# A Mamba and mixture-of-experts block on one core: another order of engines and steps in the first stage

## The reference

```
m = mean(x);  v = var(x);  xn = (x - m) / sqrt(v + eps)
```

```
logits = tokens @ Wg;  gates = softmax(logits);  idx = argmax(gates)
locations = cumsum(one_hot(idx)) - 1        # place in the expert's list; kept if < 1024
out[t] = gate[t] * (relu(tokens[t] @ W1[e] + b1[e]) @ W2[e] + b2[e])   # for kept tokens
```

## Time and profile before

| | |
|---|---|
| median of 3 runs | 1117.55 us (1115.28 to 1118.39) |
| the profiled execution's own time | 1116.6 us |
| its span, first to last instruction | 1114.8 us |
| VectorE busy | 1009.5 us (91%) |
| TensorE busy | 973.8 us (87%) |
| GpSimd busy | 880.4 us (79%) |
| ScalarE busy | 756.5 us (68%) |
| granted TensorE clock, mean | 0.939 of full speed |
| first scan of the first unit starts | 77.12 us after the span's start |

### The profile page before, as it was taken

The page is one execution under the profiler, slowest core; times in us unless marked ns, Lnnn a source line. Parts: engine busy times, 40 slices in busy tenths (PEclk is TensorE's granted clock), DMA queues, the critical chain, the costliest instruction groups (busy, mean ns, idle before and its releaser), DMA issues.

```text
span 1114.8 us, 11984 instructions
## 1 busy us (share of the span) xinstructions
PE 973.8 (87%) x3529; PEld 446.0 (40%) x3529; DVE 1009.5 (91%) x1358; ACT 756.5 (68%) x1219; POOL 880.4 (79%) x774
## 2 busy tenths in 40 slices
PE   6676777999999998989999999999899999788785
PEld 3332232444444444434444443444344444334232
DVE  5458897999999999999999999999999999999995
ACT  5655445777777868877777878678777768576331
POOL 3527888888888889798988888889889898788753
PEclk9787968999999999999999999999999999898767
DMA  9365335442342254353325324335333232945500
GB/s 275 110 152 162 79 86 128 97 101 43 84 113 64 68 116 85 76 123 76 86 48 116 80 53 114 84 76 123 85 69 81 50 85 57 216 96 113 132 29 10
DMA packets 77452, 106.99 MB, mean 96 GB/s; under 512 B 8734, under 2 KB 46540, under 8 KB 77388
## 3 DMA queue, kind: packets, MB, share of 16 engines
q1 hardware_dynamic: 72944, 97.74, 39.6%
q0 software_dynamic: 4096, 8.46, 2.2%
q10 hardware_dynamic: 348, 0.03, 0.0%
HBM read 17.99 MB, written 21.10 MB: 35 GB/s over the span
## 4 chain that ended last, share of the span: by engine, by line
PE 34%; DVE 22%; ACT 16%; issue 15%; POOL 11%; DMA 0%; POOLq 0%; DVEq 0%; ACTq 0%
DVE u_sb L1005 9%; DVE s_sb L1048 8%; PE bank L1189 5%; PE bank L1226 5%; POOL s_sb L636 5%; PE bank L1154 4%; PE bank L1134 4%; PE bank L1241 4%; PE bank L1219 4%; POOL expert_in L643 4%; ACT bank L860 3%; PE bank L1186 3%; PE bank L1145 2%; ACT L719 2%; ACT L715 2%
## 5 line engine op out<-in xcount | busy, mean ns | idle before, releaser
L636 POOL TENSOR_TENSOR s_sb<-s_sb,c_of 128x512 f32<-128x512 f32 x480 | 614.5, 1289 | 127.9 <-DVE s_sb L1048 123.2
L1048 DVE TENSOR_TENSOR_SCAN s_sb<-bank,u_sb 128x512 f32<-128x512 f32 x512 | 619.9, 1211 | 15.1 <-ACT bank L860 14.9
L860 ACT ACTIVATE bank<-bank,a_neg 128x510 f32<-128x510 f32 x512 | 332.3, 664 | 213.4 <-PE bank L1226 211.7
L1005 DVE TENSOR_TENSOR u_sb<-bank,b_of 128x512 f32<-128x512 f32 x512 | 342.5, 669 | 25.8 <-PE bank L1219 25.3
L1219 PE MATMUL bank<-dsp,sel_d 128*128 128x512 f32 x512 | 329.8, 644 | 24.6 <-DVE u_sb L1005 18.7
L1226 PE MATMUL bank<-dsp,sel_d 128*128 128x512 f32 x512 | 230.1, 449 | 50.6 <-DVE s_sb L1048 47.0
L1219 PEld LDWEIGHTS bank<-dsp,sel_d 128*128 128x128 f32 x512 | 101.2, 198 | 204.0 <-DVE u_sb L1005 108.0
L1226 PEld LDWEIGHTS bank<-dsp,sel_d 128*128 128x128 f32 x512 | 101.3, 198 | 177.4 <-DVE s_sb L1048 132.4
L1241 PE MATMUL bank<-s_sb,con 128*32 128x512 f32 x1024 | 145.1, 640 | 24.6 <-POOL s_sb L636 21.8
L1134 PE MATMUL bank<-xnT,wx 128*128 128x512 f32 x256 | 133.7, 607 | 0.0
L643 POOL DMA_INDIRECT expert_in<-xn,put_at x64 | 65.3, 1021 | 38.9 <-DVE put_at L1034 21.1
(11 more groups left out here) (140 smaller groups left out, 1032.7 us busy)
## 6 DMA issues: line engine op xcount, KB each, us to landing
b_of<-bc SPq DMA_DIRECT2D x64, 256.0 KB, 5.5
c_of<-bc SPq DMA_DIRECT2D x64, 256.0 KB, 5.8
dsp<-hi SPq DMA_DIRECT2D x64, 256.0 KB
dsp<-dd SPq DMA_DIRECT2D x64, 256.0 KB
expert_in<-fill SPq DMA_DIRECT2D x16, 260.0 KB, 5.9
xn<-expert_in SPq DMA_DIRECT2D x8, 520.0 KB, 5.3
moe<-fill SPq DMA_DIRECT2D x8, 512.0 KB, 7.1
xn<-L_ffn_W SPq DMA_DIRECT2D x16, 256.0 KB, 5.0
```

The costliest lines, as they stand in the source:

```text
L636: pool.tensor_tensor(s_now, s_now, c_of[:, hf, hh, :], ALU.mult).then_inc(S["p_ready"], 1)
L860: act.activation(d, d, ACT.Exp, scale=a_neg[:, k:k + 1]).then_inc(S["decay_ready"], 1)
L1005: dve.tensor_tensor(u_sb[:, w % U_RING, :], du_ps[w % 2][:, :], b_of[:, hf, head_of(w), :], ALU.mult).then_inc(S["u_ready"], 1)
L1048: dve.tensor_tensor_scan(s_sb[:, w % S_RING, :], decay_of(w)[:, :], u_sb[:, w % U_RING, :], 0.0, ALU.mult, ALU.add).then_inc(S["scan_done" ...
```

## The change

In the layer norm, ScalarE takes the logarithm and exponential of group 1 ahead of the first SiLUs, and those of the other groups as early as their variances allow; it norms one chunk (11) instead of five. GpSimd norms chunks 1 to 10 and 12, VectorE chunks 0 and 13 to 15. The copies of chunks 6, 8, 10, 12 and 14 to `xnT` go to VectorE. TensorE transposes one or two chunks earlier than before, and `logits(q)` waits for each chunk's copy by itself. ScalarE's exponential of the routing stands behind the second half's SiLUs. TensorE makes the two routing products ahead of the second half's bc and v tiles, and its first spreads wait for `rt_pos` (the fifth signal of `route_dve`) in place of `routed`. VectorE forms the gates' sum and reciprocal behind the integer copy of the places.

```diff
+NORM_BY = ("dve",) + ("pool",) * 10 + ("act", "pool", "dve", "dve", "dve")
+XNT_BY_DVE = (6, 8, 10, 12, 14)
+FIRST_DX = 12
...
+        def normed(j):
+            name = NORM_BY[j]
+            return S["xn_" + name], sum(NORM_BY[i] == name for i in range(j + 1))
+        def taken(j):
+            if j in XNT_BY_DVE:
+                return S["xnT_dve"], XNT_BY_DVE.index(j) + 1
+            return S["xnT_act"], sum(i not in XNT_BY_DVE for i in range(j + 1))
...
-            for g in range(1, LN_GROUPS):
-                if g == LN_GROUPS - 1:
+            for j in range(1, CHUNKS):
+                if NORM_BY[j] != "pool":
+                    continue
+                pool.wait_ge(S["rstd_ready"], [a <= j * CT for a in LN_AT].count(True))
+                for i in range(j * CT, (j + 1) * CT):
+                    ins = norm(pool, i)
+                ins.then_inc(S["xn_pool"], 1)
+                if j == FIRST_DX:
                     scale_x(0, 0)
-                pool.wait_ge(S["rstd_ready"], g + 1)
...
+                    pool.wait_ge(S["dx_ready"], 1)
+                    zero_first()
...
             act.wait_ge(S["setup_act"], 5)
+            rsqrt(1)
             silus(0, 0)
-            rsqrt(1)
+            rsqrt(2)
...
             take_bc(0, 0)
-            norm_tiles(1)
             taps(1, 5)
+            rsqrt(3)
...
-            rsqrt(2)
             evac(wo.rearrange("p k m -> p (k m)"), y_ps[:, 2 * P:4 * P], 7)
             softplus_step(0, 0, 1)
-            norm_tiles(2)
             take_xnT(1)
+            rsqrt(4)
             softplus_step(0, 0, 2)
             take_xnT(2)
-            rsqrt(3)
             softplus_step(0, 0, 3)
             take_xnT(3)
-            norm_tiles(3)
+            rsqrt(5)
             take_xnT(4)
+            take_xnT(5)
+            copy_logits(0)
+            norm_tiles(11)
             take_delta(0, 0)
-            copy_logits(0)
-            rsqrt(4)
-            take_xnT(5)
-            take_xnT(6)
-            norm_tiles(4)
             take_xnT(7)
             copy_logits(1)
-            rsqrt(5)
-            take_xnT(8)
+            split_high(0, 0)
             take_xnT(9)
-            norm_tiles(5)
-            take_xnT(10)
-            split_high(0, 0)
             take_xnT(11)
             copy_logits(2)
-            for j in range(12, CHUNKS):
-                take_xnT(j)
+            take_xnT(13)
+            take_xnT(15)
             copy_logits(3)
+            silus(0, 1)
             act.wait_ge(S["lg_read"], CHUNKS // 4)
             act.activation(rt_b, rt_a, ACT.Exp).then_inc(S["route_act"], 1)
-            silus(0, 1)
...
+            def take_xnT(j):
+                dve.wait_ge(S["xnT_pe"], j + 1)
+                dve.tensor_copy(xnT[:, SEQS * j:SEQS * (j + 1), TAPS - 1:ROW],
+                                xnT_bank(j)[:, :].rearrange("p (s t) -> p s t", s=SEQS)).then_inc(S["xnT_dve"], 1)
...
-                if g == 5:
-                    take_logits(0)
             newton(LN_GROUPS - 1)
             dve.wait_ge(S["rstd_ready"], LN_GROUPS)
-            norm_tiles(CHUNKS - 1, 2)
-            for q in range(1, 4):
-                take_logits(q)
+            norm_tiles(13, 2)
+            norm_tiles(14, 3)
+            norm_tiles(15, 4)
+            take_xnT(6)
+            take_logits(0)
+            take_xnT(8)
+            take_xnT(10)
+            take_logits(1)
+            take_xnT(12)
+            take_xnT(14)
+            take_logits(2)
+            take_logits(3)
...
-            dve.wait_ge(S["route_act"], 1)
-            link(dve.tensor_reduce(r_sum, by_e(rt_b), AX, ALU.add))
-            link(dve.reciprocal(r_sum, r_sum))
...
-            link(dve.tensor_tensor(rt_pos, du_ps[0][:, :], rt_scan, ALU.add))
-            dve.wait_ge(S["route_dve"], 4)
+            dve.tensor_tensor(rt_pos, du_ps[0][:, :], rt_scan, ALU.add).then_inc(S["route_dve"], 1)
+            dve.wait_ge(S["route_dve"], 5)
...
-            link(dve.tensor_copy(r_place, r_code))
+            dve.tensor_copy(r_place, r_code)
+            dve.wait_ge(S["route_act"], 1)
+            link(dve.tensor_reduce(r_sum, by_e(rt_b), AX, ALU.add))
+            dve.reciprocal(r_sum, r_sum)
...
             transposes(4)
+            transposes(5)
             logits(0)
+            transposes(6)
             pe.wait_ge(S["sel_ready"], 1)
             first_tile("D", 0)
-            transposes(5)
-            transposes(6)
             by_token(0)
             transposes(7)
+            transposes(8)
             logits(1)
-            transposes(8)
...
             transposes(12)
+            transposes(13)
             by_token(2)
-            transposes(13)
             transposes(14)
             transposes(15)
             logits(3)
             by_token(3)
             first_tile("z", 1)
             first_tile("x", 1)
-            first_tile("bc", 1)
-            first_tile("v", 1)
-            pe.wait_ge(S["xnT_act"], CHUNKS)
             pe.wait_ge(S["route_dve"], 4)
             pe.matmul(du_ps[1][:, :], ones, rt_hot[:, :, 0:TILES], start=True, stop=True).then_inc(S["route_pe"], 1)
             pe.matmul(du_ps[0][:, :], tri, rt_hot[:, :, 1:TILES + 1], start=True, stop=True
                       ).then_inc(S["route_pe"], 1)
-            pe.wait_ge(S["routed"], 1)
+            first_tile("bc", 1)
+            first_tile("v", 1)
+            pe.wait_ge(S["route_dve"], 5)
             for w in range(AHEAD):
                 spread(0, w)
```

More of the change, by code:

```diff
@@ L230, in bass_mamba_moe @@
             "wt_ready a_by_d_ready sel_ready setup_pe setup_act fill_zeroed fill_ready ein_filled moe_filled "
-            "xn_dve xn_act xn_pool xnT_pe xnT_act logits_pe route_dve route_act route_pe routed "
+            "xn_dve xn_act xn_pool xnT_pe xnT_act xnT_dve logits_pe route_dve route_act route_pe routed "
             "l0_ready stats_done var_ready rstd_ready ln_act lt_pe lt_act lg_read "
@@ L583, in split_low @@
                 pool.tensor_tensor(lo, dd, hi.bitcast(F32), ALU.subtract).then_inc(S["lo_ready"], 1)
-            for g in range(1, LN_GROUPS):
-                if g == LN_GROUPS - 1:
-                    scale_x(0, 0)
-                pool.wait_ge(S["rstd_ready"], g + 1)
[L589 to L595, removed]
+            for j in range(1, CHUNKS):
[6 more added lines that the diff above has]
+                if j == FIRST_DX:
+                    scale_x(0, 0)
+                    pool.wait_ge(S["dx_ready"], 1)
+                    zero_first()
             split_low(0, 0)
@@ L695, in take_xnT, with norm_tiles @@
                                ACT.Copy).then_inc(S["xnT_act"], 1)
-            def norm_tiles(g):
-                act.wait_ge(S["rstd_ready"], g + 1)
-                for i in range(LN_AT[g], LN_AT[g] + CT):
+            def norm_tiles(j):
+                act.wait_ge(S["rstd_ready"], [a <= j * CT for a in LN_AT].count(True))
+                for i in range(j * CT, (j + 1) * CT):
                     ins = act.activation(xn[:, i, :], acc[:, i, :], ACT.Identity, bias=shift[:, i:i + 1],
@@ L1083, in transposes @@
             def transposes(j):
[L1084 to L1089, removed]
+                pe.wait_ge(*normed(j))
                 if j > 3:
-                    pe.wait_ge(S["xnT_act"], j - 2)
+                    pe.wait_ge(*taken(j - 3))
                 elif j > 0:
@@ L1104, in logits @@
                     pe.wait_ge(S["lt_act"], q)
-                pe.wait_ge(S["xnT_act"], 4 * (q + 1))
                 for k in range(4):
                     j = 4 * q + k
+                    pe.wait_ge(*taken(j))
                     mm = pe.matmul(lt_ps[32 * k:32 * (k + 1), :], wg_sb[:, :],
```

## The result

The changed kernel takes 1101.07 us (median of 4 runs, 1099.94 to 1102.15) against 1117.16 of the kernel before in the same comparison (4 runs): a ratio of 0.986, 95% interval 0.9848 to 0.9872, or 16 us. The forecast was 9 us, and 1104.5 to 1113 as the range. The direction was right, the size was not.

A forecast was written before the change was run, and what follows sets the result against it. First stage taken as a relay with no leading engine, then GpSimd's scatters. x tile 6.4 us earlier and tail 2.6 bring the first scan 8.9 us earlier: 1116.6 to 1107.7, with 0.95 for the median, rounded to 1108.5; range 1104.5 to 1113.

The forecast's parts named there:

- Logarithms, scales and norms: First stage's layer norm: group 1's scale at 17.0 us instead of 21.1, and no norm late for its transposes.
- The D tile, not the norms, is next: First half's D tile: the norms' early lead yields only 1.2 us, D ending at 39.1 against 40.3.
- Relay 15.6: From the D tile's end to the second half's z tile: 15.6 us, including 2.6 for a low clock.
- T to the first scan: 9.2: From the end of the second half's x tile (T) to the first scan: 9.2 us, 2.6 better than before.
- The first scan's lead passes through: Behind the first scan: the distance to the end stays 1037.7 us, so its 8.9 us lead shortens the whole.
- the high clock: Rival: no low clock stretch behind the D tile, gain 11.5 us, 1106 us; chance 0.11.
- The other three: Rivals: low clock for more of the relay, 1112, 0.13; GpSimd's norms slowed beside VectorE, 1117, 0.06; all low clock, 1122.5, 0.04.
- the slower one: Rival: TensorE at 1.2 GHz from the D tile to the v tile, first scan 4.8 us late, 1122.5; chance 0.04.
- about 85%: In the slower rival: share of the stretch at the low clock level from which the change costs time.

The follow-up runs named there:

- e3: Kernel before with four idle matmuls of 384 columns, two behind transposes(2) and two behind transposes(3): 1115.9 us, ratio 1.0001.
- e10: Changed kernel with the routing's exponential ahead of the second half's SiLUs and the gates' sum and reciprocal ahead of the scan of places again: 1102.8 us.
- e7: Changed kernel with ScalarE norming five chunks again (1, 4, 7, 10 and 13): 1105.3 us, ratio 0.9898 to the kernel before.
- e9: Changed kernel with logits(q) waiting for all four copies before its first product, as before: 1102.3 us, ratio 0.9884 to the kernel before.
- e1: Kernel before with only the end of the stage (the tail) changed: 1113.0 us, ratio 0.997.
- e2: Changed kernel with the end of the stage (the tail) put back as before: 1103.9 us, ratio 0.9883 to the kernel before.
- e5: Kernel before with 14 idle matmuls of 384 columns in TensorE's gaps: 1112.4 us, ratio 0.9966.
- e6: Kernel before with only the logarithms of groups 1 to 5 at the changed kernel's places: 1114.8 us, ratio 0.9987.
- e8: Changed kernel with all 16 copies on ScalarE: 1103.3 us, ratio 0.9876 to the kernel before.
- e12: Changed kernel with the exponential and gates' sum early again and three idle matmuls between the second and third spread: 1100.4 us, ratio 0.9856 to the kernel before.

## Why the prediction failed, step by step

- *Logarithms, scales and norms.* Right. Group 1's Newton step at 16.17 (forecast 16.1), GpSimd's 44 tiles from 17.14 on in 19.41 us (forecast 17.0 and 0.43 a tile). No norm was late.
- *"The D tile, not the norms, is next", ending at 39.1.* This step failed, and most. Its working took TensorE's prices from the rows of before, which were taken at 1.2 GHz, for a stretch that the changed kernel ran at 2.4 GHz. The forecast was 31.4 for the start of `logits(0)`, then 1.9, 1.0 for `transposes(6)` and 4.8 for the D tile. Measured: 30.48, then 1.9, 0.5 and 3.0, so 35.89. `logits(0)` starts 0.9 us sooner by the waits by chunk and takes no less, as it waits inside for its last copy. With the forecast's own start and the prices of full clock (1.0 from e3, 0.5, 3.0) the sum is 35.9: all of the 3.2 us is the clock. With the clock at 0.51 the same stream ended the D tile at 38.00 (e10), only 1.1 below the forecast, so 2.1 of the 3.2 us are the luck of this execution.
- *Relay 15.6.* The same step failed by 3.8 us here. It put 2.6 us for a low clock ("the new order feeds TensorE with shorter gaps, so I take 2.6"). That term measured nothing: in all profiles of the new order but e7's (0.97) the clock is 1.00 from 36 to 58 us, and the relay is 11.8 wherever norms, copies and waits are those of the change. The other 1.2 us: I summed the lengths of rows, and rows of pipelined matmuls overlap. Two transposed chunks took 1.04 us where I put 1.2, and a `by_token` that doesn't wait 0.44 and not 0.66. e9 gives 0.4 of it to the waits by chunk.
- *T to the first scan: 9.2.* Nearly right, 9.4; the tail 13.88 for 13.5. e1 and e2 show its 2.35 us by themselves. One reason in it was wrong: the exponential isn't on the path (e10).
- *The first scan's lead passes through.* Right: the rest is 1036.5 against 1037.7, and 1035.8 to 1039.6 among all profiles, without a pattern that I could tie to the edits.
- *Rivals.* The nearest was the high clock (1106), which had 0.11. It was too slow still, as it kept the low clock up to the D tile and the summed rows. The other three didn't occur. In the slower one, the turning point of "about 85%" doesn't follow from its own terms: 8.5, 4.3 and 3.45 us are what the low clock costs in all, and 2.6 + 8.9 of them, 71%, would use up the gain.

What the 15.55 us ahead of the first scan are made of, by the marks:

- the tail: 2.35 us (e1, e2);
- the relay: 6.8 of hand-offs and 1.9 of clock (e5);
- up to the D tile: 1.3 to 1.7 by the new order and 2.7 to 3.1 by the clock. At the low clock the D tile starts at 34.17 in the new order (e10) and at 35.46 in the old; at the high clock it ends at 35.89 in the new and at 37.63 in the old (e3). The forecast's 1.2 for the order was about right.

That is near 10.7 us of order and 4.8 of clock (middles of the ranges). The clock's part isn't safe from run to run, as e10 shows.

The single edits account for less than the 10.7: the tail 2.35, ScalarE's norms 2.8 (e7, 1.6 and 1.2), the logarithms 1.0 (e6, relay), its copies 0.7 (e8), the waits by chunk 0.4 to 0.5 (e9), together some 7.3 us. The rest isn't isolated by any run. TensorE's own order, with its transposes one or two chunks earlier, was not tried alone, and parts that hide behind each other show nothing one at a time. The relay of the new order at a low clock occurred in no profile, so what the clock is worth there in the new order isn't known.

## What to carry to other kernels

If a change closes TensorE's gaps, don't price its matmuls by rows that were taken between those gaps: work the sum out at both clock levels and ask which one the new order will feed. In a relay of several engines, don't expect the parts to add up when each is taken back alone: here they made 7.3 of some 10.7 us. Before reading a difference of 1 or 2 us at one mark, look at how far that mark moves in profiles of the same instructions: here 2.2 us at one place and 0.01 behind it. And before shifting a step off an engine, see what that engine waits for next: ScalarE's exponential was free where it stood.

## What the runs showed of the hardware

- Matmuls whose result nobody reads made a kernel 4.0 us faster (e5, 14 of them). Four gave one execution a clock of 1.00 from 30 to 36 us, where before had 0.50, and in the median did nothing (e3).
- The same instruction stream had the clock at 0.51 (e10), 0.72 (e12) or 1.00 (after) from 30 to 36 us; the D tile's end moved by 2.1 us with it, while relay and tail repeated to 0.01 us. Where the clock falls shifts from one execution to the next.
- VectorE's `scalar_tensor_tensor` with two inputs in SBUF took 0.29 us alone (45.63, 48.54) and 1.05 and 1.10 where GpSimd ran a `tensor_tensor`. VectorE and GpSimd of the changed kernel:

```profile
37.12 1.05 DVE L963 SCALAR_TENSOR_TENSOR zs<-xs,g_sb 128x128 f32<-128x128 f32 x1
41.56 1.10 DVE L963 SCALAR_TENSOR_TENSOR zs<-xs,g_sb 128x128 f32<-128x128 f32 x1
```

```profile
36.75 1.27 POOL L588 TENSOR_TENSOR dd<-dd,xs 128x512 f32<-128x512 f32 x1 [0.20 <-ACT dd L773]
40.15 2.36 POOL L598 TENSOR_TENSOR dd<-dd,hi 128x1024 fp32r<-128x1024 f32 x1 [1.97 <-ACT hi L779]
```

  The Trainium skill ("SBUF — State Buffer", "Who interferes with whom") says that a VectorE instruction with two SBUF inputs contends with a GpSimd instruction that reads SBUF; the trace agrees. GpSimd's 44 norms ran at 0.44 us a tile beside VectorE's statistics, against 0.43 in the kernel before.
